# Second mixture-of-experts layer: expert pairs with interleaved rows, y kept in DRAM blocks, gathers per token, y stored through ScalarE's DMA queue

## The reference

```python
x = x + tanh(g_xattn[0]) * L0_xattn(ctx, layernorm(x))
x = x + tanh(g_ffn[0]) * L0_ffn(layernorm(x))            # 4 experts, token t uses expert t % 4
x = x + tanh(g_xattn[1]) * L1_xattn(ctx, masks, layernorm(x))
x = x + tanh(g_ffn[1]) * L1_ffn(layernorm(x))
# L1_ffn, T = 1024 tokens, 64 experts, TOP_K = 8, INTER = 96
probs = softmax(x @ gate_w)
top_vals, top_idx = top_k(probs, 8);  top_vals /= sum(top_vals)
g = einsum('th,ehi->tei', x, w_gate);  u = einsum('th,ehi->tei', x, w_up)
h = silu(g) * u * rw[:, :, None]                          # rw: top_vals at top_idx, 0 elsewhere
out = einsum('tei,eih->th', h, w_down)
```

## Time and profile before

| | us |
|---|---|
| median of 3 runs | 409.8 |
| lowest, highest | 408.25, 410.25 |
| profiled execution, span from first to last instruction | 409.7 |
| first scatter of rows / first unit on PE | 116.0 / 166.0 |
| last down product of the loop ends | 362.8 |
| matmuls that sum the picks | 377.1 to 407.1 |

### The profile page before, as it was taken

One profiled execution on the slowest core, in us unless ns is written; L12 is line 12 of the kernel. 1 busy time (PEld: TensorE's weight loads), 2 busy tenths in 40 slices (PEclk: granted clock), 3 DMA queues, 4 the chain that ended last, 5 costly groups with the idle time before them and its releaser, 6 DMA issues.

```text
span 409.7 us, 7438 instructions
## 1 busy us (share of the span) xinstructions
PE 289.1 (71%) x2042; PEld 234.1 (57%) x2042; DVE 231.8 (57%) x1114; ACT 138.5 (34%) x393; POOL 212.3 (52%) x257
## 2 busy tenths in 40 slices
PE   5898168127810610899876778989899977871997
PEld 1345057126810510788765666878788855541886
DVE  0799999989397472355632433565655533331352
ACT  2263354315634420244432233444444432320000
POOL 2632013013358777777777777777777774540000
PEclk9999999657975555799999899999999999975899
DMA  4899997270016633999999999749999999726991
GB/s 134 306 341 300 302 322 226 80 228 3 1 48 224 232 128 131 316 330 324 324 331 311 338 326 318 234 136 297 301 326 300 305 289 267 214 58 251 346 299 62
DMA packets 72983, 98.39 MB, mean 240 GB/s; under 512 B 13007, under 2 KB 66144, under 8 KB 71920
## 3 DMA queue, kind: packets, MB, share of 16 engines
q1 hardware_dynamic: 63728, 79.03, 63.0%
q0 software_dynamic: 9216, 18.90, 14.5%
HBM read 62.23 MB, written 39.85 MB: 249 GB/s over the span
## 4 chain that ended last, share of the span: by engine, by line
PE 44%; DVE 22%; DMA 14%; POOL 9%; issue 5%; SPq 3%; ACT 3%; DVEq 0%; POOLq 0%; ACTq 0%
PE psum L756 16%; PE psum L765 10%; POOL expert_rows L514 8%; PE psum L812 7%; DVE work L1036 5%; DMA token_picks<-down_w,target 5%; DVE top L1032 5%; PE psum L745 4%; DMA gu_w<-expert_rows 3%; DMA sim<-expert_rows 3%; DVE xn L1154 2%; DVE stats L1007 2%; PE psum L576 2%; PE psum L570 2%; DMA sim<-token_picks 1%
## 5 line engine op out<-in xcount | busy, mean ns | idle before, releaser
L765 PE MATMUL psum<-proj_t,gu_w 96*96 96x256 f32 x254 | 77.5, 387 | 5.0 <-DVE gu_w L1247 5.0
L514 POOL DMA_INDIRECT expert_rows<-x_rows,place_at x64 | 62.5, 977 | 23.8 <-issue 22.9
L534 POOL DMA_INDIRECT token_picks<-down_w,target x64 | 58.7, 917 | 25.1 <-issue 14.4
L534 POOL DMA_INDIRECT token_picks<-adj,target x63 | 57.8, 917 | 22.5 <-issue 13.7
L967 ACT ACTIVATE gu_w<-psum 96x96 f32<-96x96 f32 x127 | 31.3, 246 | 108.2 <-PE psum L756 107.7
L1247 DVE TENSOR_TENSOR gu_w<-gu_w,psum 96x96 f32<-96x96 f32 x127 | 31.6, 249 | 56.8 <-ACT gu_w L967 56.0
L756 PE MATMUL psum<-gu_w,wgu 128*96 128x96 f32 x504 | 56.0, 256 | 7.7 <-DVE gu_w L1242 7.6
L756 PEld LDWEIGHTS psum<-gu_w,wgu 128*96 128x96 f32 x504 | 49.8, 170 | 9.6 <-DVE gu_w L1242 9.3
L1242 DVE COPY gu_w<-psum 128x192 f32<-128x192 f32 x127 | 43.7, 344 | 0.0
L745 PEld LDWEIGHTS psum<-ident,gu_w 96*128 96x128 f32 x160 | 22.0, 145 | 30.0 <-issue 12.3
L745 PE MATMUL psum<-ident,gu_w 96*128 96x96 f32 x160 | 27.7, 256 | 15.0 <-DMA gu_w<-expert_rows 14.4
(11 more groups left out here) (182 smaller groups left out, 448.2 us busy)
## 6 DMA issues: line engine op xcount, KB each, us to landing
expert_rows<-empty_rows SPq DMA_DIRECT2D x1, 15360.0 KB, 69.8
wgu<-in_L_ffn_w_gate_up SPq DMA_DIRECT2D x57, 192.0 KB
proj_t<-in_L_ffn_w_down SPq DMA_DIRECT2D x113, 96.0 KB
gu_w<-expert_rows SPq DMA_DIRECT2D x80, 120.0 KB
base<-in_L_ffn_w_gate_up SPq DMA_DIRECT2D x35, 192.0 KB
sim<-expert_rows SPq DMA_DIRECT2D x48, 120.0 KB, 2.0
pen<-in_L_ffn_w_gate_up SPq DMA_DIRECT2D x21, 192.0 KB
gu_w<-in_L_ffn_gate_up_proj SPq DMA_DIRECT2D x4, 512.0 KB, 8.1
```

Of the source, the lines that this page charges most:

```text
L514: pool.indirect_dma_start(rows_dram, bass.IndirectOffsetOnAxis(ap=place_at[:, t, k:k + 1], axis=0), x_rows[:, t, :], None).then_inc(placed ...
L534: pool.indirect_dma_start(picks_dram, bass.IndirectOffsetOnAxis(ap=target[0:SLOTS, n, i:i + 1], axis=0), y_slots[n][0:SLOTS, i, :], None, ...
L765: last = pe.matmul(psum[0:SLOTS, 4 + e % 2, i * D:(i + 1) * D], h1_t[:, e % 2, i * SLOTS:(i + 1) * SLOTS], wd[:, n, :], start=True, stop=True)
```

## The change

1. *Pairs.* Two neighbouring experts make a pair; their rows are interleaved in one DRAM block (row of slot s and half h at 2s + h). One DMA loads 96 x 2 rows (2 KB per partition), and two load the weights of both experts (3 KB and 2 KB per partition), which are laid out by pair on the host. 128 units, u = 2p + h, over 64 pairs. Phase A takes the pairs 31 down to 0, phase B 0 up to 31. The weight ring holds 16 pairs, the row ring 8, the y ring 4. Phase B finds 16 pairs resident.
2. *Rows.* No tags: a row has 1024 bytes. `place_rows` loses the scan and the subtraction; ranks are counted in twos. The scatters of phase A go by ranks: the first 8 DMAs carry ranks 0 and 1 of tiles 0 to 3, the next 8 ranks 2 and 3, and so on, with one semaphore per group; pair p (p < 4) waits for group p alone. The 32 of phase B follow without a break.
3. *y in DRAM.* ScalarE stores both halves of a pair, 96 x 2 rows, by one plain DMA from its own queue after copying y of the next unit (`store_y`). The y rows of the second phase and of the leftovers (14592 rows of 1 KB) are cleared by a second big store, which SP issues right behind the first.
4. *Gathers.* GpSimd gathers per tile and rank 128 rows of y (64 indirect DMAs, ring of 8), and DVE adds each, scaled by its weight, to x3 (`add_pick`). The gathers of phase A run beside phase B, with the additions in the loop from unit 88; those of phase B begin when pair 60 is stored, 8 at a time for pairs 60, 61, 62 and 63. The diagonal matmuls, the loads of `token_picks` and `picks` buffers are gone.
5. *DVE's small work* (list of leftovers, routing weights, weights of the picks, addresses of the gathers) is cut into slices, one per unit in units 1 to 73.
6. *Leftovers* run with buffers of their own before unit 72 instead of at the end; the expert 0 of phase B is an ordinary unit now, and one chunk of the list still always runs.

```diff
-            for u in range(UNITS):
-                if u % 3 < 2 and late:
-                    b, n = late.pop(0)
-                    place_rows(b, n, n + 1)
-                scatter(u)
+            def gather(n):
+                t, k = pick_of(n)
+                if n >= G_RING:
+                    pool.wait_ge(summed, n - G_RING + 1)
+                pool.indirect_dma_start(gathered[:, n % G_RING], None, y_dram[0:Y_MAIN + Y_OVER] if t < HT else y_dram,
+                                        bass.IndirectOffsetOnAxis(ap=gather_at[:, t, k:k + 1], axis=0)).then_inc(gather_landed[n % G_RING], 16)
+            y_stored(NP - 1)
+            total_over = load_over(pool)
+            pool.wait_ge(over_landed, total_over * 16 + 1)
+            pool.wait_ge(gather_at_ready, 1)
+            for n in range(PICKS // 2):
+                gather(n)
+            for n in range(PICKS // 2, PICKS):
+                if n % (2 * HT) == 0:
+                    y_stored(PAIRS - 4 + (n - PICKS // 2) // (2 * HT))
+                gather(n)
...
+            by_pair = rows_dram[0:NR * REGION].rearrange("(e r) d -> e (r d)", e=PAIRS)
+            sp.dma_start(by_pair[:, 0:2 * CAP * D].rearrange("e (p n) -> p e n", p=CAP),
+                         empty_rows[0:CAP].rearrange("p (a n) -> p a n", a=1).to_broadcast([CAP, PAIRS, 2 * D])).then_inc(rows_cleared, 16)
+            later_y = y_dram[Y_MAIN:].rearrange("(e p h) d -> p e (h d)", p=CAP, h=2)
+            sp.dma_start(later_y, empty_rows[0:CAP].rearrange("p (a n) -> p a n", a=1).to_broadcast(list(later_y.shape))).then_inc(y_cleared, 16)
...
+            def load_rows(p):
+                n = p % X_RING
+                if p < TOP_K_EXPERTS // 2:
+                    sp.wait_ge(placed_a[p], 16 * 2 * HT)
+                if p == NP:
+                    for placed in placed_b:
+                        sp.wait_ge(placed, 16 * HB * TOP_K_EXPERTS)
+                if p >= X_RING:
+                    sp.wait_ge(xt_filled, 2 * (p - X_RING) + 2)
...
+            for p in range(PAIRS):
+                if p == OVER_AFTER - 1:
+                    sp.wait_ge(y_cleared, 16)
+                    total_over = run_over()
+                if p + X_RING < PAIRS:
+                    load_rows(p + X_RING)
...
+                if p + W_RING < PAIRS:
+                    load_weights(p + W_RING)
...
+            def copy_y(u):
+                p, h = u // 2, u % 2
+                act.wait_ge(y_filled, u + 1)
+                if h == 0 and p >= Y_RING:
+                    act.wait_ge(y_landed[p % Y_RING], 16 * (p // Y_RING))
+                act.copy(y_slots[p % Y_RING][:, h], psum[0:CAP, 4 + h, 0:D]).then_inc(y_ready, 1)
+            def store_y(p):
+                n = p % Y_RING
+                act.wait_ge(y_ready, 2 * p + 2)
+                if p == NP:
+                    act.wait_ge(y_cleared, 16)
+                act.dma_start(y_dram[y_row(p):y_row(p) + 2 * CAP].rearrange("(p h) d -> p (h d)", h=2),
+                              y_slots[n].rearrange("p h d -> p (h d)")).then_inc(y_landed[n], 16)
+            for u in range(UNITS):
+                if u == 2 * OVER_AFTER:
+                    run_over()
+                silu_gate(u)
+                if u:
+                    copy_y(u - 1)
+                if u >= 3 and u % 2:
+                    store_y(u // 2 - 1)
...
+            def find_picks(t, step):
+                if step == 0:
+                    at = place8[:, t].rearrange("p (k a) -> p k a", a=1).to_broadcast([P, TOP_K_EXPERTS, NE])
+                    link(dve.tensor_tensor(picked, of_picks(place[:, t]), at, ALU.is_equal))
+                elif step == 1:
+                    link(dve.tensor_tensor(picked_part, picked, of_picks(rw[:, t]), ALU.mult))
+                elif step == 2:
+                    link(dve.tensor_reduce(pick_w[:, t], picked_part, mybir.AxisListType.X, ALU.add))
...
+            def add_pick(n):
+                t, k = pick_of(n)
+                dve.wait_ge(gather_landed[n % G_RING], 16 * (n // G_RING + 1))
+                need(dve, summed, n - HT + 1)
+                dve.scalar_tensor_tensor(out=x3[:, t], in0=gathered[:, n % G_RING], scalar=pick_w[:, t, k:k + 1], in1=x3[:, t],
+                                         op0=ALU.mult, op1=ALU.add).then_inc(summed, 1)
```

More of the change, by code:

```diff
@@ L185, in gated_layers_kernel @@
[L185 to L193, removed]
@@ L530, in scatter @@
-            def scatter(e):
-                n = e % Y_RING
-                pool.wait_ge(y_ready, e + 1)
-                for i in range(SUBS):
-                    pool.indirect_dma_start(picks_dram, bass.IndirectOffsetOnAxis(ap=target[0:SLOTS, n, i:i + 1], axis=0),
-                                            y_slots[n][0:SLOTS, i, :], None, bounds_check=T * TOP_K_EXPERTS - 1, oob_is_err=False).then_inc(scattered[n], 16)
-            late = [(b, n) for b in (2, 3) for n in range(PICKS)][8:]
@@ L749, in gate_up1, with transpose_slots @@
-            def gate_up1(e):
-                n = units[e][1] % W_RING
-                pe.wait_ge(xt_copied, e + 1)
-                pe.wait_ge(w_landed[n], w_count[e])
-                need(pe, h_ready, e - 1)
+            def transpose_slots(u):
+                p, h = u // 2, u % 2
+                if h == 0:
+                    pe.wait_ge(x_landed[p % X_RING], 16 * (p // X_RING + 1))
+                need(pe, xt_copied, u - 1)
+                for k in range(KC):
+                    last = pe.transpose(psum[:, h, k * CAP:(k + 1) * CAP], x_slots[p % X_RING][:, h, k * P:(k + 1) * P],
+                                        ident[0:CAP, 0:CAP])
+                last.then_inc(xt_filled, 1)
@@ L758, in gate_up1, with down1 @@
                 last.then_inc(gu_filled, 1)
-            def down1(e):
-                n = units[e][1] % W_RING
-                pe.wait_ge(h_ready, e + 1)
-                need(pe, y_ready, e - 1)
-                for i in range(SUBS):
-                    last = pe.matmul(psum[0:SLOTS, 4 + e % 2, i * D:(i + 1) * D], h1_t[:, e % 2, i * SLOTS:(i + 1) * SLOTS], wd[:, n, :],
-                                     start=True, stop=True)
-                last.then_inc(y_filled, 1)
+            def down1(u):
+                p, h = u // 2, u % 2
+                pe.wait_ge(h_ready, u + 1)
+                need(pe, y_ready, u - 1)
+                pe.matmul(psum[0:CAP, 4 + h, 0:D], h1_t[:, h], wd[w_slot(p)][:, h], start=True, stop=True).then_inc(y_filled, 1)
@@ L1118, in place_rows @@
                 dve.wait_ge(chosen_ready, b + 1)
-                dve.wait_ge(consts_ready, 10)
-                for t in tiles:
-                    last = dve.tensor_tensor_scan(order[:, t], chosen[:, t], zeros[:, 0:NE], 0.0, ALU.add, ALU.add)
-                link(last)
-                for t in tiles:
-                    dve.tensor_scalar(x_rows[:, t, D:ROW].bitcast(U32), order[:, t], -1.0, token_end[:, t:t + 1], ALU.mult, ALU.add)
+                dve.wait_ge(consts_ready, 11)
                 filled(F_RANK[b])
@@ L1219, in _ @@
-            link(dve.scalar_tensor_tensor(out=over_of[:, 1:2], in0=over_of[:, 0:1], scalar=float(REGION), in1=over_of[:, 1:2], op0=ALU.mult, op1=ALU.add))
-            link(dve.tensor_scalar(over_of[:, 4:5], over_of[:, 0:1], float(NE), -float(NE), ALU.is_ge, ALU.mult))
-            link(dve.tensor_tensor(over_of[:, 0:1], over_of[:, 0:1], over_of[:, 4:5], ALU.add))
-            for n in range(3):
-                last = dve.tensor_scalar(over_diag[:, n], ident[:], over_of[:, n:n + 1], None, ALU.mult)
@@ L1289 @@
+            for n in range(PICKS // 2, PICKS):
+                add_pick(n)
 _INS = ["x", "ctx_512", "mask_SxS2_bk1", "mask_BxS2_bf0", "g_xattn", "g_ffn", "L0_xattn_Wq", "L0_xattn_Wk",
```

702 lines of the change are left out of this document (373 added, 329 removed).

## The result

The changed kernel takes 413.2 us in the median of 20 runs (409.4 to 420.4), the kernel before beside it 410.2 (406.6 to 412.6): a ratio of 1.007, 95% interval 1.004 to 1.010. It is slower by a little under 1%. The forecast was 377, the range 366 to 398, and slower had a chance of 0.08: the prediction was wrong by 36 us. The profiled execution of the changed kernel has a span of 412.2 us, 2.5 more than before's.

The account below looks back on a forecast made before the run. The bound differed by stage; GpSimd scatters and DMAs held expert units above PE's 1.28 us. Unit 6 at 164.0, plus 156.2, 1.3, 0.8, 5.5, 2 and 4, gives 333.8; a 43 us tail gives 376.8, forecast 377, range 366 to 398.

Parts of the forecast that it names:

- Start of the stage: Start of the expert units: unit 6 begins at 164.0 us, set by the first 32 scatters landing and a row load.
- I take 0: Before unit 6: clears and weights finish in time; units 0 to 5 slip 0 us, up to 2 at the lower rate.
- Rival D: Start: pairs do not start early, weights late behind the 14.9 MB clear, rows delayed in SP's queue; 387 us, chance 0.06.
- rival A: Expert stage: the DMA engines stay the bound, with a few us of buffer stalls; 390 us, chance 0.17.
- The stage: Unit 6 to the last down product: 122 units at PE's 1.28 us, 156.2 us, plus additions, ending at 333.8 us.
- The DMA term: Expert stage: uneven DMA load, 18.9 MB to move before pair 23 starts; 4 us taken of 0 to 7.
- clock and list matmul: Expert stage on PE: 1.3 us for the colder clock at the start, 0.8 for the list matmul at unit 13.
- DVE's find_picks: Units 27 to 66: one 0.752 us operation each puts DVE at 1.34 us against 1.28; 2 us taken, bounds 0 to 6.
- the leftover chunk: Now in the middle of the expert stage rather than at the end: adds 5.5 us on PE.
- The tail: After the last down product: 32 late gathers 1.265 us apart, last add and output store; about 43 us.
- B: Expert stage: a store's issue on ScalarE is dear, gain gone at 1.31 us each; 452 us at the 1.98 bound, chance 0.06.
- C: Tail and units 96 to 119: a gather is dearer on GpSimd; 396 us at 1.6 us each, chance 0.05.

Follow-up runs that it names:

- e10: e7 with first-phase weights issued 9 pairs ahead of use instead of 16: 389.9 us, ratio to before 0.955.
- e2: Changed kernel with the y clear covering only the leftover chunks' blocks, 8.65 MB in place of 14.9: 400.2 us, ratio to before 0.981.
- e5: Like e2, but leftover blocks of only 4 x 96 rows, so a 0.39 MB clear (measurement only): 401.0 us, ratio to before 0.978.
- e11: Changed kernel with both clears written from 128 partitions in place of 96, same bytes, queue and order: 400.7 us, ratio to before 0.979.
- e6: Kernel before with a 14,592 KB clear of an unread tensor added behind the clear of expert_rows: 419.1 us, ratio to before 1.025.
- e7: e2 with VectorE's first sum behind unit 96 instead of 88, holding the early gathers back: 395.7 us, ratio to before 0.967.
- e4: Changed kernel with the 64 stores of y issued from SyncE's queue instead of ScalarE's: 421.8 us, ratio to before 1.032.

## Why the prediction was wrong

35.4 us lie between the sum, 376.8, and the profiled span. They come from three of its steps. The 33 us that were forecast had three parts too: an earlier unit 6 (175.1 on PE before, 164.0 forecast), 11 us; the stage, 18; the tail, 4. The first came out with the other sign.

**Start of the stage, forecast 164.0, measured 187.8: +23.8.** This is the step that failed. It had the clear end at 88 to 112 us, by dividing 29.2 MB by the rates of other stretches, 304 and 407 GB/s. It ended at 16.7 + 122.9 = 139.6, a mean near 236 GB/s for these 29.2 MB. Until 100 us the engines kept the lower of the two rates (294 to 319 GB/s); what was wrong is the end, which ran at 127 to 207. I had the slow end of a clear in front of me, in the trace of before between 70 and 82 us (99 GB/s at a share of 0.34), and took none of it into the rate. The page of before even has its price:

```profile
expert_rows<-empty_rows SPq DMA_DIRECT2D x1, 15360.0 KB, 69.8
```

15.7 MB in 69.8 us are 225 GB/s, and at this rate the 27.5 MB of both clears end at about 138 (139.6 measured). The issue of the weights hung behind the clear to 125.6, and the rows, which follow the weights in SyncE's order, were issued from 162.8 on. "I take 0" cost 20.7 us: 187.8 less the 167.1 at which PE begins unit 6 in e10 (167.12 in its timeline, where silu follows at 168.64). e2 and e5 show the clear as the cause by leaving part of it out, e11 by making it quick, e6 by adding it to the kernel before, with 10 us there. The other 3.1 are the scatters' floor, 167.1 for 164: rows are scattered, landed, loaded and transposed at half clock a little slower than I added up. Rival D named exactly this and was given 10 us and 0.06; by its own mechanism it was worth 20.7. Its sign, unit 0 after 160, was seen, and so was A's, PE waiting over 10 us for rows (43.6).

**The stage, forecast 169.8 from unit 6 to T, measured 177.8: +8.0.** The DMA term was 4 and is 3.7 + 9.9 = 13.6, +9.6. I had budgeted the first stretch, units 6 to 46, well (3.7), but not the second: weights, rows and stores are 0.49 MB a unit in units 64 to 95, 384 GB/s at 1.28 us, and the early gathers follow straight on them. e7 shows the gathers' share: 5.6 of e2's 10.4 go with them (2.9 to 5.6 over the four traces with this edit). That is rival A, in another place than I looked, and smaller. The other terms: clock and list matmul 0.7 for 2.1; DVE's find_picks 0.0 for 2, so neighbours do overlap; the leftover chunk 6.7 for 5.5; the last unit 0.8 for nothing. Together 8.2, 0.2 over what there is to explain.

**The tail, forecast 43, measured 46.6: +3.6.** The gathers were right: the first late one at 362.7, T - 2.8 for T - 2, and 1.25 us apart for 1.265. The last landed and was added by 405.5, its store by 407.5; the end of the program came at 412.1. The rows after T are those of the engines' final drains:

```profile
L91 POOLq DRAIN  x1: 16910/16910/16910, 395.0 to 395.0; - x1
...
L91 SPq DRAIN  x1: 13/13/13, 407.5 to 407.5; - x1
```

GpSimd's ends at 395.0 + 16.9 = 411.9, 10.2 us after its last gather starts at 401.74. Up to the landing of the last store the tail is 42 us, 1 less than forecast; the sum had no term for the drain.

**Rivals B and C** are settled against. A store on ScalarE takes 0.323 us in the median and 0.407 at most: below the 0.43 taken and far from the 1.31 from which it would decide. The Trainium skill's page Perfetto Trace Analysis (DMA Instruction — HWDGE) has one generator lock for the issuing sequencers; by a lock held for SyncE's 0.43 us, stores here would show up to 0.86. None of the 64 does, though 49 of them overlap an issue of SyncE in the timelines, so this trace gives that price no support. A gather takes 0.947 us, for the 0.962 of the scatter.

So the likeliest mechanism did happen in the stage, which is 9.9 us shorter, but "nearly all of the gain is the stage" left out that the gain had to pass a start set by the clear.

## What to carry to other kernels

A large store at the head of an in-order queue is priced to its last packet, not at the rate of its middle: find when the one in the trace landed, and what hung behind it, before it is called hidden. Once PE holds its pace, add up the bytes per unit for each stretch of the loop, prefetches and gathers too, and compare with what the engines move when full; weights asked for 16 pairs ahead held up rows that were needed at once. And when a start is brought forward, look for the next thing that sets it (here the scatters): past that point a cheaper cause buys nothing, and part of the gain is given back to loads that now run beside the work.

## What the runs showed of the hardware

- While two broadcast stores from 96 partitions ran, the engines moved 305 GB/s at a DMA share of 0.93, with a slow end (127 GB/s at 0.36); with the same bytes from 128 partitions they moved 396 at 1.06. With the edit of these two stores the changed kernel takes 3% less.
- An issue behind two large clears in one queue hung for 62.8 us, and then the next ones took 0.4 to 4.5.
- GpSimd's final drain ended 10.1 to 10.2 us after the start of its last gather in the changed kernel, e4, e7 and e10 (411.9, 421.1, 392.6 and 386.7 us), and so sets their end. In the kernel before it ended by 378.4, hidden under 30 us of other work.
